# Staging slots and maxima for each kind of attention, one piece of the maxima at a time, and a new order for the last two passes

## What is computed

```
h1 = ln(x);  x = softmax(q1 k1^T / 4) v1 @ o1_w + o1_b + x      (keys: the 512 tokens)
h2 = ln(x);  x = softmax(q2 k2^T / 4) v2 @ o2_w + o2_b + x      (keys: 1601 context rows)
h3 = ln(x);  a, g = split(h3 @ ff_w1 + ff_b1);  x = (a * gelu(g)) @ ff_w2 + ff_b2 + x
```

## Time and profile before

| | us |
|---|---|
| three timed runs | 3695.53 median (3688.76 to 3696.15) |
| the profiled execution, its own time | 3690.11 |
| its span, first to last instruction | 3688.3 |

### The profile page before, as it was taken

One profiled execution on the slowest core, in us unless ns is written; L12 is line 12 of the kernel. 1 busy time (PEld: TensorE's weight loads), 2 busy tenths in 40 slices (PEclk: granted clock), 3 DMA queues, 4 the chain that ended last, 5 costly groups with the idle time before them and its releaser, 6 DMA issues.

```text
span 3688.3 us, 43767 instructions
## 1 busy us (share of the span) xinstructions
PE 3235.1 (88%) x16320; PEld 1493.1 (40%) x16320; DVE 2080.8 (56%) x2565; ACT 1989.5 (54%) x3806; POOL 620.7 (17%) x676
## 2 busy tenths in 40 slices
PE   5887888998899989999899988999988988887877
PEld 2333333343353434534344433544344534433435
DVE  5555565665555765557555655556755665455511
ACT  1543565656655656456664566545665566354531
POOL 2231121203102120112202132021210031001001
PEclk8987988999998999999999888999999999998989
DMA  6434335333433243332443445323333243222202
GB/s 156 140 90 97 95 89 141 89 82 88 126 89 108 68 107 94 95 96 53 130 107 87 120 119 147 97 90 72 92 92 87 46 101 90 63 43 47 69 24 71
DMA packets 194515, 340.88 MB, mean 92 GB/s; under 512 B 19384, under 2 KB 101696, under 8 KB 193024
## 3 DMA queue, kind: packets, MB, share of 16 engines
q1 hardware_dynamic: 194304, 338.08, 35.5%
HBM read 202.29 MB, written 114.75 MB: 86 GB/s over the span
## 4 chain that ended last, share of the span: by engine, by line
PE 60%; DVE 14%; DMA 11%; ACT 6%; POOL 3%; issue 3%; SPq 3%; DVEq 0%; ACTq 0%; POOLq 0%
DVE mx L933 12%; PE pr L1124 11%; PE po L1141 11%; PE pd L1105 7%; PE pf L1049 5%; PE pf L996 5%; PE pf L1060 5%; DMA QS<-scr_q 5%; PE pf L1019 3%; PE pf L1037 3%; ACT ET L852 3%; PE pf L1028 3%; DMA scr_k<-HS 2%; PE pf L1052 2%; DMA raw<-ff_w_dram 1%
## 5 line engine op out<-in xcount | busy, mean ns | idle before, releaser
L852 ACT ACTIVATE ET<-pr 128x512 f32<-128x512 f32 (+1 forms) x2720 | 1478.1, 596 | 1372.5 <-PE pr L1124 1356.8
L933 DVE TENSOR_REDUCE mx<-pd 128x2 f32<-128x804 f32 (+2 forms) x1600 | 1569.4, 1033 | 1004.2 <-PE pd L1105 1001.7
L1124 PE MATMUL pr<-QS,KS 64*128 64x512 f32 (+1 forms) x2720 | 871.0, 514 | 86.6 <-ACT ET L852 84.1
L1105 PE MATMUL pd<-KS,QS 64*128 64x400 f32 (+2 forms) x3200 | 636.2, 396 | 160.0 <-DVE mx L933 85.4
L1141 PE MATMUL po<-ET,V 128*32 128x512 f32 (+2 forms) x5440 | 770.2, 640 | 1.2 <-ACT OU L858 1.2
L1124 PEld LDWEIGHTS pr<-QS,KS 64*128 64x128 f32 (+1 forms) x2720 | 337.4, 189 | 962.7 <-ACT ET L852 648.5
L1105 PEld LDWEIGHTS pd<-KS,QS 64*128 64x128 f32 x3200 | 361.1, 197 | 302.9 <-DVE mx L933 194.0
L743 POOL TENSOR_TENSOR HS<-uT,HS 128x512 fp32r<-128x512 f32 (+4 forms) x168 | 189.9, 1131 | 762.5 <-ACT uT L816 762.5
L759 POOL TENSOR_TENSOR OA<-OA,DEN 128x512 f32<-128x512 f32 (+1 forms) x48 | 60.8, 1267 | 1259.5 <-DVE DEN L941 1259.5
L1049 PE MATMUL pf<-HS,WS 128*128 128x512 f32 x730 | 217.7, 430 | 50.1 <-DVE uT L926 17.8
L1019 PE MATMUL pf<-cT,w_kv 96*128 96x400 f32 (+3 forms) x384 | 168.3, 564 | 31.5 <-ACT uT L816 30.6
(11 more groups left out here) (82 smaller groups left out, 2186.0 us busy)
## 6 DMA issues: line engine op xcount, KB each, us to landing
WS<-parts SPq DMA_DIRECT2D x160, 320.0 KB, 2.9
KS<-scr_k SPq DMA_DIRECT2D x80, 600.8 KB, 10.6
QS<-scr_q SPq DMA_DIRECT2D x80, 512.0 KB, 10.2
scr_k<-HS SPq DMA_DIRECT2D x144, 200.0 KB
scr_q<-HS SPq DMA_DIRECT2D x96, 256.0 KB
KS<-scr_k SPq DMA_DIRECT2D x80, 192.0 KB, 3.7
scr_k<-HS SPq DMA_DIRECT2D x48, 256.0 KB
OA<-OU SPq DMA_DIRECT2D x320, 32.0 KB
```

Of the source, the lines that this page charges most:

```text
L852: activation(ET[0:q.rows[k], s % 2, 2 * pair + e, :], pr[e][0:q.rows[k], :], ACT.Exp).then_inc(score_free, 1)
L933: v.reduce_max(mx[:, t, 2 * p:2 * p + 2, c], pd[no % 2][:, :, 0:cols], AX_X).then_inc(unit_free, 1)
L1105: ins = mm(pd[no % 2][:, e, 0:cols], queries[:, t * P:(t + 1) * P], keys, start=True, stop=True)
L1124: mm(pr[e][0:m, :], keys, queries, start=True, stop=True).then_inc(score_ready, 1)
```

## The change

`QS` keeps three slots, but where both kinds run, two of them go to the cross groups in turn and one to the self groups. The maxima have a buffer for each kind (`mx1`, `mx2`), and their units are laid out for each kind by itself, so that units of a cross and of a self group can alternate. A unit waits for the copies of the maxima only where a turn lies between it and the unit before; the turn waits until all units before it are reduced. The turn of a cross group stands 3 places ahead of its first score, not 5. The steps behind a group are nearer in the first two phases (`..._ALONE`). The order of the side work changes: t3 comes one v2a fill earlier, n1 ahead of all of the remaining v2a fills; ff2 of pass 5 moves from phase 6 to the head of phase 7; phase 6 is dealt by steps, and in phase 7 n3 is mixed into v2b.

```
     elif c == N - 1:
-        first, rest = gate(c - 1, 3)
-        seq = places("v2b", c) + mixed(places("o2", c - 1), []) + places("n3", c - 1) + places("t3", c - 1)
-        seq += places("g", c - 1) + [first] + rest
+        first, rest = gate(c - 1, 4)
+        seq = places("ff2", c - 2) + places("o2", c - 1) + mixed(places("v2b", c), places("n3", c - 1))
+        seq += places("t3", c - 1) + places("g", c - 1) + [first] + rest
...
-            seq += behind[:2] + places("t3", c - 1) + places("g", c - 1) + [first] + rest
-            behind = behind[2:]
+            seq += behind[:1] + places("t3", c - 1) + places("g", c - 1) + [first] + rest
+            behind = behind[1:]
+        if i is None:
+            seq = [p for p in seq if p[0] != "ff2"]
         if c + 3 < N:
-            behind = mixed(behind[:2], places("n1", c + 3)) + behind[2:]
+            behind = places("n1", c + 3) + behind
...
+            _last = {s: max([p.end for p in GROUPS if p.slot == s], default=0) for s in range(SLOTS)}
+            _own = [p.slot for p in GROUPS if p.kind == _kind and (_kind == "C" or p.step0 >= 2 * G * TT)]
+            if _kind == "C" and _crosses >= 2:
+                _slot = _own[-2]
+            elif _kind == "S" and _own:
+                _slot = _own[-1]
+            else:
+                _slot = min(_last, key=_last.get)
...
-    _over = [p.n for p in GROUPS[:_q.n] if p.n <= _q.n - RING or p.shares_keys(_q)]
+    _over = [p.n for p in GROUPS[:_q.n] if p.slot == _q.slot or p.shares_keys(_q)]
...
 COPY, MOVE, INVERT, DIVIDE = 5, 8, (14, 15, 16, 17), 18
+MOVE_ALONE, INVERT_ALONE, DIVIDE_ALONE = 6, (9, 10, 11, 12), 13
...
+def deal_by_steps(stretches, steps):
+    slots, kinds = [], []
+    for stretch in stretches:
+        works = [p[0] for p in stretch if p[0] in STAGE]
+        if works and works[0] in SHORT and slots and kinds[-1] == works[0] and len(slots[-1]) == 1:
+            slots[-1].append(stretch)
...
-        _behind = [b for b in _odd if b > 4 * _from + DIVIDE]
+        _behind = [b for b in _odd if b > 4 * _from + DIVIDE_ALONE + 2]
...
+    elif _c == N - 2:
+        deal_by_steps(_all, range(_from + 1, _to))
...
-    _from = max(_at + 7, _free, 0)
-
+    _alone = _q.end <= 2 * G * TT
+    _from = max(_at + (8 if _q.kind == "S" else 11), _turn[_q.kind] + 3, 0)
+    if _alone:
+        _from = max(_at + 7, _turn["S"] + 2, 0)
     _lag = 5 if 4 * _q.step0 - _from >= 24 else 3
-    _to = 4 * _q.step0 - _lag - (4 if _lag == 5 else 2)
+    _to = 4 * _q.step0 - _lag - 2
     if _q.kind == "S":
-        _to = min(_to, _from + 8)
-    _beats = [b for b in range(_from, _to) if b % 2 == 0]
+        _to = min(_to, _from + (8 if _alone else 16))
+    _beats = [b for b in range(_from, _to) if b % 2 == 0 and b + 1 not in TURN_AT and b - 1 not in TURN_AT]
...
-        mx = sb("mx", [P, TT, HG, len(CHUNKS)])
+        mx = {"S": sb("mx1", [P, TT, HG, 1]), "C": sb("mx2", [P, TT, HG, len(CHUNKS)])}
...
-                if u == 0 and q.n:
-                    pe.wait_ge(max_copied, HG * q.n)
+                elif TURNS_BEFORE[no] > TURNS_BEFORE[no - 1]:
+                    pe.wait_ge(max_copied, HG * TURNS_BEFORE[no])
...
-            def turn_maxima(q):
+            def turn_maxima(q, units):
+                pe.wait_ge(unit_free, units)
                 pe.wait_ge(max_steps, 3 * (q.n + 1))
```

More of the change, by code:

```diff
@@ L136, with __init__ @@
 class Group:
-    def __init__(self, n, kind, i, g, step0, unit0, at):
+    def __init__(self, n, kind, i, g, step0, at, slot, uses):
         self.n, self.kind, self.i, self.g = n, kind, i, g
@@ L167 @@
                 _at, _selves = JP + T * (_selves % 3) if _c is None else 2 * JP, _selves + 1
-            GROUPS.append(Group(len(GROUPS), _kind, _pass, _g, _q.end if _q else 0,
-                                _q.unit0 + len(_q.units) if _q else 0, _at))
+            GROUPS.append(Group(len(GROUPS), _kind, _pass, _g, _q.end if _q else 0, _at, _slot,
+                                sum(p.slot == _slot for p in GROUPS)))
     PHASE_STEPS.append((_from, GROUPS[-1].end))
 STEP = [(q, k) for q in GROUPS for k in range(q.kt)]
-UNIT = [(q, u) for q in GROUPS for u in range(len(q.units))]
 LAST_OF = {(q.kind, q.i): q for q in GROUPS}
@@ L209, in deal @@
         k += any(p[0] in STAGE for p in stretch)
+SHORT = ("t1", "t2", "t3", "tc")
+def deal_by_steps(stretches, steps):
[4 more added lines that the diff above has]
+            slots[-1].append(stretch)
+        elif slots and kinds[-1] is None:
+            slots[-1][-1] = slots[-1][-1] + stretch
+            kinds[-1] = works[0] if works else None
+        else:
+            slots.append([stretch])
+            kinds.append(works[0] if works else None)
+    assert len(slots) <= len(steps)
+    for k, slot in enumerate(slots):
+        for n, stretch in enumerate(slot):
+            PLACES.setdefault(4 * steps[k * len(steps) // len(slots)] + 1 + 2 * n, []).extend(stretch)
 for (_c, _i), (_from, _to) in zip(PHASES, PHASE_STEPS):
@@ L288, in split_for @@
     return max(fills, key=lambda p: SPLIT[p])
-STAGE_AT, UNITS_AT, TURN_AT, = {}, [0] * BEATS, {}
-_free = 0
+STAGE_AT, UNITS_AT, TURN_AT = {}, {b: [] for b in range(BEATS)}, {FIRST_BEAT: GROUPS[0]}
+_turn = {"S": FIRST_BEAT, "C": FIRST_BEAT}
 for _q in GROUPS:
@@ L462, in blocks_kernel @@
         gelu_done = sem("gelu_done")
-        staged = [sem(f"staged{r}") for r in range(RING)]
+        staged = [sem(f"staged{r}") for r in range(SLOTS)]
         unit_ready = sem("unit_ready")
@@ L516, in score_rows @@
             rows = slice(ROWS * e, ROWS * e + ROWS)
-            return KS[rows, p, q.at + n0:q.at + n0 + cols], QS[rows, q.ring, p, :]
+            return KS[rows, p, q.at + n0:q.at + n0 + cols], QS[rows, q.slot, p, :]
         def stored_through(count):
@@ L874, in _ @@
                     beside(*p)
[L875 to L876 removed]
+                if ended(beat, COPY, COPY):
+                    take_sums(ended(beat, COPY, COPY))
         @block.vector
@@ L965, in _ @@
                     set_key_rows()
-                    for u in range(len(GROUPS[0].units)):
-                        reduce(GROUPS[0], u)
+                    for no in range(len(GROUPS[0].units)):
+                        reduce(no)
                 if beat in TURN_AT:
@@ L970, in _ @@
                 if 0 <= beat < BEATS:
-                    for no in range(UNITS_BEFORE[beat], UNITS_BEFORE[beat] + UNITS_AT[beat]):
-                        reduce(*UNIT[no])
-                for part, behind in enumerate(INVERT):
-                    if ended_slot(beat, behind):
-                        invert(ended_slot(beat, behind), part)
+                    for no in range(UNITS_BEFORE[beat], UNITS_BEFORE[beat] + len(UNITS_AT[beat])):
+                        reduce(no)
+                for part, behind in enumerate(zip(INVERT, INVERT_ALONE)):
+                    if ended_slot(beat, *behind):
+                        invert(ended_slot(beat, *behind), part)
         @block.tensor
@@ L1149, in _ @@
                 if beat == FIRST_BEAT:
-                    for u in range(len(GROUPS[0].units)):
-                        unit(GROUPS[0], u)
+                    for no in range(len(GROUPS[0].units)):
+                        unit(no)
                 if beat in TURN_AT:
-                    turn_maxima(TURN_AT[beat])
+                    turn_maxima(TURN_AT[beat], UNITS_BEFORE[max(beat, 0)])
                 if 0 <= beat < BEATS:
@@ L1156, in _ @@
                         scores(s, r // 2)
-                    for no in range(UNITS_BEFORE[beat], UNITS_BEFORE[beat] + UNITS_AT[beat]):
-                        unit(*UNIT[no])
+                    for no in range(UNITS_BEFORE[beat], UNITS_BEFORE[beat] + len(UNITS_AT[beat])):
+                        unit(no)
                 if r == 3 and 1 <= s <= len(STEP):
```

77 lines of the change are left out of this document (42 added, 35 removed).

## The result

The change makes the kernel slower. Its median is 3788.4 us against 3695.8 before, a ratio of 1.0239 with an interval of 1.0174 to 1.0305; the same kernel timed again later gave 1.0264 (1.0238 to 1.0289). The profiled execution took 3780.4 us for a span of 3778.6, at a mean clock of 0.924 (before: 0.931).

The account below looks back on a forecast made before the run. The prediction took PE, busy 88% of the span, to be bound by its waits and low clock. Its terms summed to -104 us, from 3690.1 to 3586; set against the runs' median it gave 3589 us, range 3515 to 3680.

Parts of the forecast that it names:

- two rivals on the other side: Slower through sums behind the cross transfer (3758 to 3764 us, 0.07); or little effect, within 7 us of 3692 (0.05).
- rival 3: Sums land after the whole cross transfer, DVE stands at the inversions, PE stops: +68 us, 3758 to 3764 us; chance 0.07.
- Units one by one: Middle phases: spreading units over even places saves time beside feed-forward fills, -12 us (between 0 and -43).
- (b): t3 8 places behind the last key store, not 12, makes ACT wait for stores: +3 us (0 to +26).
- Term (a): Cross transfer issued ahead of the group's sums on SP's queue, so DVE's inversions wait: +8 us (0 to +40).
- Staging: Earlier cross transfers cut PE's query waits: cross groups -20 us (0 to -20.4), self groups -10 us (0 to -39.7).
- -15 for the clock: Low clock behind the query waits that go: PE regains -15 us (between 0 and -45).
- Cross staging: Last phases: first units 12 places behind their staging, not 8, so query waits shrink: -20 us (between 0 and -20.4).
- the clock behind it: Low clock of 17.0 us behind the second POOL wait goes: -8 us.
- The turn: Cross groups' turn 3 places ahead: fewer score waits for exponentials, -15 us (0 to -30), and low clock, -12 (0 to -25).
- Normalisation: New order of n1 and n3 gives POOL time, so PE's 9.1 and 10.8 us waits go: -18 us (0 to -20).
- First phases: Division comes 5 places earlier, so a 4.5 us wait of o1 goes: -5 us (0 to -7).

Follow-up runs that it names:

- e2: The changed kernel with units of cross groups moved out of the even places 14 to 20 behind a self group's end: 3639.6 us, ratio 0.9847.
- e7: e6 with the turn of every cross group 5 places ahead of its first score again, not 3: 3620.3 us, ratio 0.9804.
- e3: The changed kernel with t3 one v2a fill later again, 12 places behind the last key store, not 8: 3744.4 us, ratio 1.0122.
- e6: The changed kernel with the changes of e2 and e3 together: 3598.7 us, ratio 0.9749.
- e4: The kernel before with only the new order of the side work; units, turns, slots and staging as before: 3693.4 us, ratio 1.0005.
- e9: e1 with cross groups staged as late as in the kernel before: 3693.3 us, ratio 1.0001.
- e1: The changed kernel with units and cross groups' turns of the six middle phases back at their old places: 3657.6 us, ratio 0.989.
- e8: e6 with cross groups staged 4 places later, behind the last key store: 3595.4 us, ratio 0.9738.

## Why the prediction was wrong

It forecast 3589 us with 0.88 for faster; the kernel took 3788. Its range did not hold the time, and of its two rivals on the other side rival 3 had the sign and neither the place nor the main cause.

**The step that failed: "Units one by one".** The prediction priced a moved unit by averages over half steps of the kernel before and took it to cost the same wherever it lands; the bounds were 0 and -43 us, so a loss was left out without a reason. But those averages come from places where the old plan did put units. It had kept places 16 to 20 free, right behind the two units of place 14, and there DVE inverts. The earlier trace rows shows such work for a cross group: four inversions, 3.38 us, with reductions queued behind. That row was used to price the sums' arrival, not the units. The right question was what DVE does at the even places that get a unit for the first time. By the lists of the two plans they are 40 in a middle phase (10 others lose theirs; the prediction's 30 is the difference). Over the four half steps from place 14 the old plan gave DVE two reductions of 1.03 us and four inversions of 0.91, together 5.7 us; the new one gives it nine reductions and the same inversions, 12.9 us. Before, these four half steps took 9.9 us where there are inversions; after, they take 15.9. Nine reductions alone are 9.3 us, about as long as the half steps, so the pairs without inversions lose less (8.7 to 11.1). Price: 149 us (e2), 111 of it at place 18. The value of the spreading itself, -12 in the sum, is nothing that can be measured by e2 and e7: what the straight line of the earlier trace rows had said.

**The second: term (b), t3.** Put at +3 (0 to +26), it measured 44 us (e3), and 41 where there is no collision (e6 against e2, medians of two chips). The prediction did look at the one old t3 at 8 places, but it took the landing of the stores from a trace in which the cross transfer was issued behind them. Term (a) moved that transfer ahead of the stores; (b) was priced as if it had not. ACT's wait for the key stores shows that the two act together: with t3 at 8 places it is 13.6 and 12.1 us under the old staging (e4, e9), and 45.0 and 40.7 under the new one (after, e1). What t3 costs in time under the old staging is open, since e4's middle phases are 31 us longer with t3 and n1 moved at once.

**Without these two the sum comes near, in part by luck.** It was -104 us; e6, in which both are repaired, is 88 us below its kernel before. But terms that were too small and terms that were too large stand against each other:
- *Staging.* Cross waits of the last phases went whole, 17.1 us, as said. Self waits fell by 16.5 us (39.7 to 23.2), more than the 10 taken and inside the bounds. (A step of the last phase is longer than the 4.1 us of the prediction: 3504.2 is the first score of the last group, so 267.0 us are 52 steps of 5.1 us, and the four places cover the 4.4 us whole.) For the middle phases -10, a third of the -15 for the clock and +8 for term (a) were taken, some -7 us; e9 against e1 gives 36, in the profiled executions most of it in PE's busy time. The ring-order rule of the Trainium skill ("DMA: Bandwidth & Descriptors", section "Queues, rings and completion order"), as the prediction read it, would have made the self term nil. With the transfers behind it moved away and the stores left, it was not: 34.3 against 21.0 us of waits. The prediction's own rows had a sign of it, 5.4 us with a cross transfer behind and 4.4 with nothing beside.
- *Last two phases.* Cross staging (-20), two thirds of the clock (-10), POOL (some -10) and the clock behind it (-8) come to some -48 us there. They are 24 us shorter, and e4, which has only the new order and still 21.5 us of query waits in them, is 29 us shorter. So the gain measured there is the order's, and what the 17.1 us of cross waits gave in time is not shown.
- *The turn.* -15 and -12 were taken, e7 gives 22: the size is right, the mechanism is not shown. The waits behind the 40 turns hardly fell, from 29.8 to 27.3 us: those behind the first scores fell to 9, but 37 of the first scores now stand before they start, 17 us in all and up to 0.61 each. Over the 15 us around the first scores of the eight phases with cross groups the mean clock rose from 0.78 to 0.87. But the turn isn't shown to be the cause: in e6 it is 0.85, and in e7, with the turn 5 places ahead again, 0.87. Where e7's 22 us come from stays open.
- *Normalisation.* The waits went as said. What they gave in time can't be read from e4, which moves all the order at once: -29 us in the last two phases, +31 in the middle ones. The prediction had no loss for n1 ahead of v2a.
- *First phases.* The second is 8 us shorter, for -5 taken.
- *Sums behind the transfer.* DVE's waits for them rose from 30.3 to 56.9 us; +8 was taken, and no run shows what it cost in time. Weight chunks behind the transfer (15.5 to 24.3 us) were not foreseen.

Two windows of 15 us at phase starts, of the second and the sixth phase with both kinds, first of the kernel before, where both are low:

```profile
757.90:772.90 15.00, 14.26 (x50) 5.64 (x51) 2.76 (x4) 7.82 (x15) 1.26 (x1) 0.66 0.80 181
2478.80:2493.80 15.00, 12.48 (x42) 4.36 (x42) 3.31 (x4) 7.69 (x15) 1.26 (x1) 0.66 0.80 197
```

and the same two after, where the first has gone and the second has stayed:

```profile
765.70:780.70 15.00, 10.58 (x56) 4.33 (x56) 8.52 (x10) 9.49 (x19) 2.53 (x2) 0.98 0.49 153
2586.30:2601.30 15.00, 13.26 (x50) 5.26 (x50) 8.11 (x10) 8.21 (x17) 2.52 (x2) 0.66 0.54 168
```

What stays open: of the 44 us at place 8 the self queries' waits are 13, but how much of e9's 36 us hangs on them, and how much on the key stores and the fills that no longer meet the cross transfer, no run parts.

## What to carry to other kernels

A gap in an order written out by hand can be cover for something. Before filling it, list what every engine that works in order does at that place, above all the one that is "only 56% busy", and price the item at its new place, not by its average. When two parts of a change touch the same queue, price the second against the order that the first leaves behind: with t3 at its closer place ACT waited 13.6 us for key stores under the old staging and 45.0 with the transfer moved ahead. And read a result of "no change" by phases before calling a part free: e4's was 31 us of loss and 29 of gain.

## What was not expected of the hardware

A transfer that is issued behind another can still make it late. The queries, keys and stores ahead are the same in e9 and e1; the cross transfer goes right behind the self transfer in e9 and one group earlier in e1. The self queries land 7.5 us after their issue in e9 and 6.3 in e1 (means of 30), and are waited for 34.3 and 21.0 us.

The price of short stops is not a fixed multiple of their length. The prediction took them to cost about double. From the kernel before to the one after PE's idle time grew by 51 us and its busy time by 39 for the same instructions, which fits. But in e3 36 us less of idle time came with no less busy time, in e1 against e9 8 us less came with 43 less, and in e8 26 us less of the scores' waits gave no time that can be measured.
